# Routing work moved to the end of each step, and residual rows gathered for the last six output tiles

## The chip, the cores and the metric

The kernel runs on one core of a Trainium2 chip. The metric is the device time of one execution in microseconds; three runs were taken. A core has five engines with queues of their own: PE (matrix products, into the PSUM banks), ACT (scalar functions and copies), DVE (elementwise and reductions), POOL (here above all the indirect DMAs, which gather or scatter rows by a list of indices) and SP (which only starts DMAs). They meet at semaphores: an instruction can raise one when it ends, and a queue can wait until one has reached a value. Each queue works strictly in the order in which it is written, so what stands behind a waiting instruction waits too.

## The reference

The input is x of 32 x 64 rows of 128 floats (2048 rows). Three blocks are each added to the residual x:

```python
x = x + xattn(layernorm(x), ctx_1024, ctx_1024, mask, ...)      # 16 heads, 128 context rows
x = x + attn(layernorm(x), A, Wb, bb, Wc, bc, Wd, bd, ...)      # a cumulative-sum recurrence, 32 hidden
x = x + ffn(layernorm(x), routers, W1, W2)                      # 4 layers over a shared pool of 16 experts

def _unipool_layer(xt, router, W1, W2):
    logits = xt @ router                       # (2048, 16)
    probs = softmax(logits)
    w, idx = max(probs), argmax(probs)
    # for each of the 16 experts: silu(xt @ W1[e]) @ W2[e], kept where idx == e, times w
```

W1[e] is 128 x 512 and W2[e] is 512 x 128. The four layers of the last block run one after the other, each with its own router; there is no residual between them. Only the sum at the very end adds the residual.

## The kernel before

Attention fills the span up to about 150 us and the recurrence the stretch up to about 190 us; the change touches neither. The rest is the expert block.

**Tiles, pieces and steps.** Each layer holds the 2048 rows sorted by expert in 16 tiles of 128. A tile that straddles two experts is computed once for each, so the loop runs over `PIECES` = 16 + 15 = 31 pieces (one tile with one expert each). `piece_steps` calls `step(i)` for i = 0 to 32 on every engine. Piece j passes through a pipeline: in step j ACT copies the expert's W1 into a staging buffer (L587); in step j+1 PE multiplies it with the tile (L915, "the hidden product" below), ACT takes the tanh (L599), DVE forms the gated hidden rows (L1300, "h(j)" below); in step j+2 PE multiplies by W2 (L933) and DVE adds the result into the tile's rows, weighted by whether the piece counts (L1316, "y(j)" below). Both products use two banks in turn: the hidden product of piece j needs h(j-2) done, and the second product of piece j needs y(j-2) done. Tile t is final after y(t+15).

**Routing beside it.** In layers 0 to 2 the finished tiles are already routed for the next layer. In step i PE transposes tile i-18 (L883, which waits for y(i-3)), ACT copies it out (L575), and PE multiplies with the router (L851). The 16 tiles are routed in five parts of 4, 3, 3, 3 and 3 tiles. `ending(k)` names the part whose last tile is k. For each part come: `largest` on DVE (L1155, L1159) at the end of the step in which its last tile's router product comes; `exponentials` on ACT (L557, one small instruction for each tile) in the step after; `choose` and `weigh` on DVE (L1167 to L1179, seven instructions); `ranks` on PE (L834, L847, which count rows of each expert); `put` on DVE (L1194 to L1197), which gives each row its place; and then POOL scatters the part's tiles into `expert_rows` in DRAM (L389). `ranks` of a part also waits for `put` of the part before. Parts 0 to 3 fall into the steps; part 4 comes after them. The parts' `exponentials`, `choose` and `weigh` stand in steps 22, 25, 28 and 31, their `ranks` and `put` in steps 23, 26, 29 and 32.

**Between the layers.** After the last `put`, DVE works out the sources of the sorted rows, and POOL gathers them tile by tile (L406) once all scatters have landed.

**The end.** In layer 3 nothing is routed. `finish(t)` on DVE (L1288) in step t+17 multiplies the finished tile by its gate into `yrows[0]`, and POOL adds its 128 rows into the output with one scatter each (L430, `compute_op=ALU.add`); the residual was stored into the output earlier by one plain DMA.

**SP.** Before the expert block SP clears 12 of the 16 parts of `expert_rows`; the last four (4 MB) it clears in layer 0, once 8 tiles of that layer have been transposed (`sp.wait_ge(s["xT_mm"], NT // 2)`).

Of the kernel before, what the change touches and what calls it, by code (L numbers as in the profile page):

```python
# [10 lines left out]
ALU = mybir.AluOpType  # L11
# [11 lines left out]
def perceiver_block(nc, x, ctx, mask, Wq, bq, Wk, bk, Wv, bv, Wo, bo, A, Wb, bb, Wc, bc, Wd, bd,  # L23
# [18 lines left out]
    FIRST = 4  # L42
    PARTS = [(0, 4), (4, 7), (7, 10), (10, 13), (13, 16)]
# [15 lines left out]
    with ExitStack() as stack:  # L59
# [3 lines left out]
        def sem(name):  # L63
            return stack.enter_context(nc.semaphore(name))
# [105 lines left out]
        scored = [sem(f"scored{r}") for r in range(4)]  # L170
        gathered = [sem(f"gathered{t}") for t in range(NT)]
# [40 lines left out]
        def ending(tile):  # L212

            return [b for b, (a, z) in enumerate(PARTS) if z - 1 == tile]

# [25 lines left out]
        def _(sp):  # L241
# [33 lines left out]
            sp.wait_ge(s["xT_mm"], NT // 2)  # L275
# [6 lines left out]
        def _(pool):  # L282
# [138 lines left out]
            def finish_rows():  # L421

                for t in range(NT):
                    pool.wait_ge(gathered[t], L * 16)
                g.tensor_copy(token_i[:], xin[:, :, ID]).then_inc(s["token_ready"], 1)
                pool.wait_ge(s["token_ready"], 1)
                pool.wait_ge(s["x2_stored"], 16)
                for t in range(NT):
                    pool.wait_ge(s["out_row"], t + 1)
                    g.indirect_dma_start(  # L430
                        out=out_rows, out_offset=bass.IndirectOffsetOnAxis(ap=token_i[:, t:t + 1], axis=0),
                        in_=yrows[0][:, t, 0:D], in_offset=None, compute_op=ALU.add).then_inc(s["out_scattered"], 16)
                pool.wait_ge(s["out_scattered"], 16 * NT)
# [13 lines left out]
        def _(act):  # L447
# [123 lines left out]
            def evac_yT(layer, t):  # L571
                act.wait_ge(s["yT_mm"], layer * NT + t + 1)
                if t >= 2:
                    act.wait_ge(s["logits_done"], (layer + 1) * NT + t - 1)
                a.copy(yT[:, t % 2, :], banks[0][:, 0:P]).then_inc(s["yT_evac"], 1)  # L575

            def one_layer(layer):
# [3 lines left out]
                def step(i):  # L581
# [9 lines left out]
                    if routes:  # L591
                        for b in ending(i - 19):
                            exponentials(layer + 1, b)
# [7 lines left out]
                    if routes and 0 <= i - 18 < NT - 1:  # L601
                        evac_yT(layer, i - 18)

# [11 lines left out]
        def _(pe):  # L615
# [252 lines left out]
            def one_layer(layer):  # L868
# [26 lines left out]
                def step(i):  # L895
# [27 lines left out]
                    if routes:  # L923
                        for b in ending(i - 20):
                            ranks(r, b)
# [10 lines left out]
                    if routes and 0 <= i - 18 < NT - 1:  # L936
                        logits_y(i - 18)

# [13 lines left out]
        def _(dve):  # L952
# [324 lines left out]
            def one_layer(layer):  # L1277
# [7 lines left out]
                def finish(t):  # L1285

                    dve.wait_ge(s["y_ready"], count(t + E))
                    v.tensor_scalar(yrows[0][:, t, 0:D], yrows[layer % 2][:, t, 0:D], xin[:, t, GATE:GATE + 1], None,  # L1288
                                    ALU.mult).then_inc(s["out_row"], 1)

                def step(i):
# [10 lines left out]
                    if routes:  # L1302
                        for b in ending(i - 19):
                            choose(r, b)
                            weigh(r, b)
                        for b in ending(i - 20):
                            put(r, b)
# [10 lines left out]
                    if routes:  # L1318
                        for b in ending(i - 18):
                            largest(r, b)  # L1320
                    elif 0 <= i - 17 < NT:
                        finish(i - 17)

                piece_steps(step)
                if routes:
                    largest(r, 4)
                    choose(r, 4)
                    weigh(r, 4)
                    put(r, 4)
# [42 lines left out]
```

## Time and profile before

| | us |
|---|---|
| median of 3 runs | 589.2 |
| lowest and highest run | 586.32, 591.73 |
| the profiled execution | 582.74 |
| its span, first to last instruction | 581.0 |
| mean granted PE clock of the profiled execution | 0.930 |
| busy PE, DVE, ACT, POOL | 492.7, 337.3, 294.8, 193.6 |

The profiled execution was itself quicker than the three timed runs. The span is 1.7 us less than its device time. A clock of 1.00 is 2.4 GHz, 0.50 is 1.2 GHz.

### The profile page before, as it was taken

What the parts mean: (1) busy time and instruction counts of PE and PEld (TensorE: products, weight loads), DVE (VectorE), ACT (ScalarE), POOL (GpSimd) and SP (SyncE); (2) the same over time, 40 slices, a digit from 0 to 9 for tenths busy, and PEclk for the clock granted to TensorE, in tenths of its full rate; (3) what the DMA queues carried; (4) which work ended last, traced back from release to release, by engine and by line L of the source; (5) the groups of instructions that cost most, each with busy time, mean ns of one, the idle gap of its engine ahead of it and who ended that gap; (6) DMA issues with size and microseconds to landing.
All of it is one profiled execution on the core that took longest, in us unless ns stands there. A gap on an engine that the chain in (4) does not pass through costs nothing.

```text
span 581.0 us, 16450 instructions
## 1 busy us (share of the span) xinstructions
PE 492.7 (85%) x5865; PEld 417.4 (72%) x5865; DVE 337.3 (58%) x912; ACT 294.8 (51%) x785; POOL 193.6 (33%) x238
## 2 busy tenths in 40 slices
PE   1689999999788879898778999787799887889992
PEld 1367777777655639897773998774699786479991
DVE  3467877787558674444436654555455445465672
ACT  1277776777571526554421665440466543166660
POOL 8342333231030035302235530233551042563385
PEclk9999999999898789998877999896899989799996
DMA  5643223300089734500001100000110000111143
GB/s 141 184 121 94 64 79 94 94 3 4 3 317 387 265 94 143 214 1 20 16 26 36 43 17 2 20 29 23 44 34 6 3 33 15 34 46 27 11 38 27
DMA packets 39052, 41.43 MB, mean 71 GB/s; under 512 B 5056, under 2 KB 26944, under 8 KB 38976
## 3 DMA queue, kind: packets, MB, share of 16 engines
q1 hardware_dynamic: 31024, 30.68, 16.1%
q0 software_dynamic: 5888, 8.63, 6.7%
q10 hardware_dynamic: 2064, 1.08, 0.7%
q8 instruction: 51, 0.84, 0.6%
q14 instruction: 25, 0.20, 0.1%
HBM read 16.65 MB, written 23.72 MB: 69 GB/s over the span
## 4 chain that ended last, share of the span: by engine, by line
PE 57%; DVE 16%; POOL 8%; issue 7%; ACT 7%; DMA 3%; DVEq 1%; ACTq 0%; POOLq 0%
PE bank L933 17%; PE bank L915 14%; PE bank L710 6%; PE bank L691 4%; POOL out_dram L430 4%; PE bank L669 3%; DVE pp L1300 2%; ACT pp L599 2%; DVE ppT L1045 2%; DVE yrows L1316 2%; PE bank L663 1%; DMA xin<-expert_rows,source_i 1%; PE bank L650 1%; PE bank L639 1%; PE bank L883 1%
## 5 line engine op out<-in xcount | busy, mean ns | idle before, releaser
L1300 DVE SCALAR_TENSOR_TENSOR pp<-pp,bank 128x512 f32<-128x512 f32 x124 | 85.2, 687 | 109.5 <-ACT pp L599 109.5
L933 PE MATMUL bank<-w,pp 128*128 x992 | 143.0, 290 | 4.4 <-issue 2.3
L915 PE MATMUL bank<-vm,ppT 128*128 x992 | 140.5, 286 | 0.1
L933 PEld LDWEIGHTS bank<-w,pp 128*128 128x128 f32 x992 | 127.7, 201 | 10.1 <-issue 7.4
L915 PEld LDWEIGHTS bank<-vm,ppT 128*128 128x128 f32 x992 | 125.5, 198 | 1.1 <-issue 0.6
L599 ACT ACTIVATE pp<-bank 128x512 f32<-128x512 f32 x124 | 74.2, 598 | 98.0 <-PE bank L915 98.0
L389 POOL DMA_INDIRECT expert_rows<-yrows,place_i x48 | 46.6, 972 | 150.4 <-DVE place_i L1197 140.3
L587 ACT COPY ppT<-w 128x512 f32 x124 | 76.6, 618 | 35.6 <-DVE piece_tile L1264 31.6
L492 ACT ACTIVATE pp<-bank,nmax 128x128 f32<-128x128 f32 x256 | 67.8, 424 | 0.0
L406 POOL DMA_INDIRECT xin<-expert_rows,source_i x48 | 46.2, 963 | 37.2 <-PE bank L904 25.7
L1316 DVE SCALAR_TENSOR_TENSOR yrows<-bank,wpiece,yrows 128x128 f32 x124 | 43.1, 347 | 24.4 <-PE bank L933 18.9
L764 PE MATMUL bank<-trib,onesb 128*128 128x512 bf16 x192 | 53.0, 438 | 0.0
L1030 DVE TENSOR_REDUCE nmax<-bank 128x4 f32<-128x512 f32 x64 | 41.0, 684 | 11.4 <-PE bank L669 11.4
L691 PE MATMUL bank<-ident,pp 128*128 128x128 f32 x256 | 40.8, 282 | 7.3 <-DVE ppT L1045 5.7
L331 POOL TENSOR_TENSOR qm<-qT,own_head 128x256 f32<-128x256 f32 x32 | 18.9, 613 | 83.3 <-ACT kT L482 83.3
L764 PEld LDWEIGHTS bank<-trib,onesb 128*128 128x128 bf16 x192 | 21.0, 112 | 25.9 <-issue 10.4
L691 PEld LDWEIGHTS bank<-ident,pp 128*128 128x128 f32 x256 | 27.4, 141 | 14.7 <-ACT pp L492 8.5
L500 ACT COPY ppT<-bank 128x512 f32<-128x512 f32 x32 | 18.9, 589 | 33.6 <-PE bank L691 33.6
L883 PE MATMUL bank<-ident,yrows 128*128 128x128 f32 x48 | 15.4, 320 | 20.6 <-DVE yrows L1316 20.6
L406 POOL DMA_INDIRECT xin<-token_rows,source_i x16 | 15.5, 969 | 51.6 <-DVE source_i L1244 39.2
L430 POOL DMA_INDIRECT out_dram<-yrows,token_i x16 | 25.0, 1560 | 16.2 <-DVE yrows L1288 11.6
L575 ACT COPY yT<-bank 128x128 f32<-128x128 f32 x48 | 12.8, 267 | 29.7 <-PE bank L883 29.7
(205 smaller groups left out, 653.7 us busy)
## 6 DMA issues: line engine op xcount, KB each, us to landing
expert_rows<-zero_rows SPq DMA_DIRECT2D x16, 1056.0 KB, 11.7
w<-in_L_ffn_W_dram SPq DMA_DIRECT2D x32, 256.0 KB, 3.4
cx<-in_ctx_dram SPq DMA_DIRECT2D x16, 128.0 KB, 2.5
token_rows<-yrows ACTq DMA_DIRECT2D x1, 1056.0 KB, 6.7
out_dram<-xs SPq DMA_DIRECT2D x1, 1024.0 KB, 13.9
xs<-in_x_dram SPq DMA_DIRECT2D x1, 768.0 KB, 5.7
expert_rows<-yrows,place_i POOLq DMA_INDIRECT x48, 2.3
xin<-expert_rows,source_i POOLq DMA_INDIRECT x48, 2.6
```

Source lines behind the costliest of these rows:

```text
L389: g.indirect_dma_start(out=region, out_offset=bass.IndirectOffsetOnAxis(ap=place_i[:, t:t + 1], axis=0), in_=yrows[(r + 1) % 2][:, t, :], ...
L406: g.indirect_dma_start(out=xin[:, t, :], out_offset=None, in_=token_rows if layer == 0 else region, in_offset=bass.IndirectOffsetOnAxis(ap ...
L430: g.indirect_dma_start(out=out_rows, out_offset=bass.IndirectOffsetOnAxis(ap=token_i[:, t:t + 1], axis=0), in_=yrows[0][:, t, 0:D], in_off ...
L492: last = a.activation(pp[:, r, k * T:(k + 1) * T], banks[r][:, k * T:(k + 1) * T], ACT.Exp, bias=nmax[:, r, k:k + 1], scale=1.0)
L587: a.copy(w1_piece[:, i % 2, :], w1[:, ds(e * FF, FF)]).then_inc(s["w1_staged"], 1)
L599: a.activation(th[:, j % 2, :], banks[2 + j % 2][:, :], ACT.Tanh, scale=0.5) \
L691: last = nc.tensor.transpose(bank[:, k * P:(k + 1) * P], pp[:, r, k * P:(k + 1) * P], ident[:])
L764: mm(bank[:, :].rearrange("p (k t) -> p k t", k=4), onesb[:], trib[:].unsqueeze(1).broadcast_to([P, 4, P]), start=True, stop=True)
L915: last = mm(banks[2 + j % 2][:, c * P:(c + 1) * P], w1_piece[:, j % 2, c * P:(c + 1) * P], xT[:, ds(tile_of[j] * P, P)], start=True, stop= ...
L933: last = mm(banks[6 + j % 2][:, 0:D], hh[:, j % 2, c * P:(c + 1) * P], w2[:, ds(e * FF + c * P, P)], start=(c == 0), stop=(c == FC - 1))
L1300: v.scalar_tensor_tensor(hh[:, j % 2, :], th[:, j % 2, :], 1.0, banks[2 + j % 2][:, :], ALU.add, ALU.mult).then_inc(s["h_ready"], 1)
L1316: v.scalar_tensor_tensor(sorted_tile, banks[6 + j % 2][:, 0:D], wpiece[:, j:j + 1], sorted_tile, ALU.mult, ALU.add).then_inc(s["y_ready"], 1)
```

## The change

Three things change.

1. In the steps of layers 0 to 2 the routing operations move to the end of the step. On ACT `exponentials` goes behind the tanh and the copy of the transposed tile. On DVE `choose` and `weigh` go behind y, and `put` goes behind them and one step later (steps 24, 27, 30; for part 3, behind the last step). On PE `ranks` goes behind the second product and the router's product.
2. In layer 3, tiles 10 to 15 (`ADDED` = 10): POOL gathers each tile's residual rows from the output into `yrows[0]`, each gather after y(t-1) and all before the first scatter. `finish` adds them (one scalar_tensor_tensor in place of the tensor_scalar), and the tile's scatter writes without adding. Tiles 0 to 9 are as before.
3. SP waits for 14 transposes in place of 8 before it clears the last four parts.

```diff
+    ADDED = NT - 6
@@ sync
-            sp.wait_ge(s["xT_mm"], NT // 2)
+            sp.wait_ge(s["xT_mm"], NT - 2)
@@ gpsimd, finish_rows
-                for t in range(NT):
+                for t in range(ADDED, NT):
+                    pool.wait_ge(s["y_ready"], (L - 1) * PIECES + t)
+                    g.indirect_dma_start(
+                        out=yrows[0][:, t, 0:D], out_offset=None, in_=out_rows,
+                        in_offset=bass.IndirectOffsetOnAxis(ap=token_i[:, t:t + 1], axis=0)) \
+                        .then_inc(x2_gathered[t], 16)
+                for t in range(ADDED):
                     pool.wait_ge(s["out_row"], t + 1)
                     g.indirect_dma_start(
...
+                for t in range(ADDED, NT):
+                    pool.wait_ge(s["out_row"], t + 1)
+                    g.indirect_dma_start(
+                        out=out_rows, out_offset=bass.IndirectOffsetOnAxis(ap=token_i[:, t:t + 1], axis=0),
+                        in_=yrows[0][:, t, 0:D], in_offset=None).then_inc(s["out_scattered"], 16)
@@ scalar, step(i)
-                    if routes:
-                        for b in ending(i - 19):
-                            exponentials(layer + 1, b)
                     if 0 <= i - 1 < PIECES:
...
                     if routes and 0 <= i - 18 < NT - 1:
                         evac_yT(layer, i - 18)
+                    if routes:
+                        for b in ending(i - 19):
+                            exponentials(layer + 1, b)
@@ tensor, step(i)
-                    if routes:
-                        for b in ending(i - 20):
-                            ranks(r, b)
                     if 0 <= i - 2 < PIECES:
...
                     if routes and 0 <= i - 18 < NT - 1:
                         logits_y(i - 18)
+                    if routes:
+                        for b in ending(i - 20):
+                            ranks(r, b)
@@ vector, finish(t)
+                    if t >= ADDED:
+                        dve.wait_ge(x2_gathered[t], 16)
+                        v.scalar_tensor_tensor(yrows[0][:, t, 0:D], yrows[layer % 2][:, t, 0:D],
+                                               xin[:, t, GATE:GATE + 1], yrows[0][:, t, 0:D], ALU.mult, ALU.add) \
+                            .then_inc(s["out_row"], 1)
+                    else:
...
@@ vector, step(i)
-                    if routes:
-                        for b in ending(i - 19):
-                            choose(r, b)
-                            weigh(r, b)
-                        for b in ending(i - 20):
-                            put(r, b)
                     if 0 <= i - 2 < PIECES:
...
                     if routes:
                         for b in ending(i - 18):
                             largest(r, b)
+                        for b in ending(i - 19):
+                            choose(r, b)
+                            weigh(r, b)
+                        for b in ending(i - 21):
+                            put(r, b)
...
                 piece_steps(step)
                 if routes:
+                    put(r, 3)
                     largest(r, 4)
```

DVE's queue before, steps 22 and 23 of layer 0, from h(21) (L1300) through `choose` and `weigh` to h(22) and the first instruction of `put`; L223 loads the tile's number into a register for the y that follows:

```order
L1300 SCALAR_TENSOR_TENSOR pp<-pp,bank 128x512
L1167 TENSOR_REDUCE mx<-ex 128x4
L1168 TENSOR_TENSOR eq<-ex,mx 128x64
L1170 SCALAR_TENSOR_TENSOR nth<-not_first,eq 128x64
L1171 SCALAR_TENSOR_TENSOR ohb<-nth,eq 128x64
L1177 TENSOR_REDUCE sm<-ex 128x4
L1178 RECIPROCAL sm<-sm 128x4
L1179 SCALAR_TENSOR_TENSOR yrows<-mx,sm 128x4
L223 TENSOR_LOAD piece_tile
L1316 ISA
L1316 SCALAR_TENSOR_TENSOR yrows<-bank,wpiece,yrows 128x128
L1300 SCALAR_TENSOR_TENSOR pp<-pp,bank 128x512
```

The same place now (line numbers are those of the changed kernel, h is L1319 and y is L1329):

```order
L1319 SCALAR_TENSOR_TENSOR pp<-pp,bank 128x512
L225 TENSOR_LOAD piece_tile
L1329 ISA
L1329 SCALAR_TENSOR_TENSOR yrows<-bank,wpiece,yrows 128x128
L1180 TENSOR_REDUCE mx<-ex 128x4
L1181 TENSOR_TENSOR eq<-ex,mx 128x64
L1183 SCALAR_TENSOR_TENSOR nth<-not_first,eq 128x64
L1184 SCALAR_TENSOR_TENSOR ohb<-nth,eq 128x64
L1190 TENSOR_REDUCE sm<-ex 128x4
L1191 RECIPROCAL sm<-sm 128x4
L1192 SCALAR_TENSOR_TENSOR yrows<-mx,sm 128x4
L1319 SCALAR_TENSOR_TENSOR pp<-pp,bank 128x512
```

y(20) stood behind the seven instructions and now stands ahead of them; h(22) now follows them directly.

DVE's queue before at the end of layer 0: the `put` of part 3 (L1194 to L1197), y(30), then `largest` of part 4:

```order
L1194 TENSOR_TENSOR rk<-bank,ohb 128x48
L1196 TENSOR_REDUCE place<-rk 128x3
L1197 CAST place_i<-place 128x3
L223 TENSOR_LOAD piece_tile
L1316 ISA
L1316 SCALAR_TENSOR_TENSOR yrows<-bank,wpiece,yrows 128x128
L1155 TENSOR_REDUCE nmx<-bank 128x3
L1159 TENSOR_TENSOR nmx<-nmx,xin 128x3
```

The same place now:

```order
L225 TENSOR_LOAD piece_tile
L1329 ISA
L1329 SCALAR_TENSOR_TENSOR yrows<-bank,wpiece,yrows 128x128
L1207 TENSOR_TENSOR rk<-bank,ohb 128x48
L1209 TENSOR_REDUCE place<-rk 128x3
L1210 CAST place_i<-place 128x3
L1168 TENSOR_REDUCE nmx<-bank 128x3
L1172 TENSOR_TENSOR nmx<-nmx,xin 128x3
```

The last y of the layer no longer stands behind the `put` of part 3.

## Rows read from the trace of the kernel before

**Rows 1.** DVE in order of time, layer 1, steps 21 and 22: start, duration, engine, line.

```profile
359.10 0.69 DVE L1300 SCALAR_TENSOR_TENSOR pp<-pp,bank 128x512 f32<-128x512 f32 x1 [1.28 <-ACT pp L599]
...
362.11 0.69 DVE L1300 SCALAR_TENSOR_TENSOR pp<-pp,bank 128x512 f32<-128x512 f32 x1 [1.68 <-ACT pp L599]
362.71 0.21 DVE L1167 TENSOR_REDUCE mx<-ex 128x4 f32<-128x64 f32 x1
...
364.70 0.35 DVE L1316 SCALAR_TENSOR_TENSOR yrows<-bank,wpiece,yrows 128x128 f32 x1 [0.39 <-issue]
```

**Rows 2.** ACT in order of time, the same steps.

```profile
358.47 0.60 ACT L599 ACTIVATE pp<-bank 128x512 f32<-128x512 f32 x1 [1.00 <-PE bank L915]
...
359.11 0.63 ACT L587 COPY ppT<-w 128x512 f32 x1
360.46 1.13 ACT L557 ACTIVATE ex<-bank,nmx,xin 128x16 f32<-128x16 f32 x4 [0.72 <-DVE nmx L1159]
```

**Rows 3.** PE in order of time, layer 1, steps 21 to 24.

```profile
357.30 1.14 PE L915 MATMUL bank<-vm,ppT 128*128 x8
358.27 0.27 PE L883 MATMUL bank<-ident,yrows 128*128 128x128 f32 x1
358.44 1.15 PE L933 MATMUL bank<-w,pp 128*128 x8
...
359.57 1.14 PE L915 MATMUL bank<-vm,ppT 128*128 x8
...
365.11 0.33 PE L883 MATMUL bank<-ident,yrows 128*128 128x128 f32 x1 [1.44 <-DVE yrows L1316]
...
365.72 1.15 PE L933 MATMUL bank<-w,pp 128*128 x8
...
366.85 2.04 PE L915 MATMUL bank<-vm,ppT 128*128 x8
```

**Rows 4.** Stretches: length, busy (instructions) of PE, PEld, DVE, ACT, POOL; clock, DMA share.

```profile
260.50:296.01 35.51, 30.24 (x226) 27.96 (x224) 16.61 (x58) 16.13 (x43) 9.74 (x10) 0.86 0.06 20
359.10:391.29 32.19, 27.26 (x226) 24.81 (x224) 16.72 (x59) 16.12 (x43) 9.74 (x10) 0.95 0.07 23
455.81:489.46 33.65, 28.71 (x226) 26.41 (x224) 16.56 (x58) 16.13 (x43) 9.74 (x10) 0.90 0.07 22
379.33:388.54 9.21, 7.73 (x73) 6.98 (x71) 5.08 (x19) 4.79 (x13) 2.84 (x4) 1.00 0.07 22
323.72:342.68 18.96, 18.96 (x173) 18.96 (x172) 11.94 (x30) 12.70 (x31) 9.54 (x10) 1.00 0.14 34
228.50:242.20 13.70, 11.42 (x88) 10.15 (x87) 5.23 (x11) 7.28 (x16) 4.39 (x6) 1.00 0.91 334
```

**Rows 5.** The same view, from h(30) to y(30) in layers 0, 1, 2.

```profile
296.01:302.00 5.99, 3.54 (x30) 3.31 (x29) 2.86 (x13) 0.39 (x2) 0.97 (x1) 0.72 0.01 3
391.29:397.28 5.99, 3.51 (x30) 3.31 (x29) 2.86 (x13) 0.39 (x2) 0.96 (x1) 0.74 0.00 0
489.46:495.09 5.63, 3.20 (x30) 2.98 (x29) 2.86 (x12) 0.39 (x2) 0.97 (x1) 0.83 0.00 0
```

**Rows 6.** In order of time, the end of layer 1: the last two `put` and POOL's last scatters.

```profile
395.73 0.17 DVE L1197 CAST place_i<-place 128x3 int32<-128x3 f32 x1
...
402.98 0.97 POOL L389 DMA_INDIRECT expert_rows<-yrows,place_i  x1 [3.29 <-DVE place_i L1197]
```

**Rows 7.** In order of time, POOL and DVE at the end of layer 3.

```profile
546.34 1.65 POOL L430 DMA_INDIRECT out_dram<-yrows,token_i  x1 [11.62 <-DVE yrows L1288]
...
574.32 1.55 POOL L430 DMA_INDIRECT out_dram<-yrows,token_i  x1 [0.30 <-issue]
...
544.00 0.29 DVE L1288 TENSOR_SCALAR yrows<-yrows,xin 128x128 f32<-128x128 f32 x1
...
570.55 0.32 DVE L1288 TENSOR_SCALAR yrows<-yrows,xin 128x128 f32<-128x128 f32 x1
```

**Rows 8.** DMA issues of the page: out, in, queue, count, us from issue to landing.

```profile
expert_rows<-yrows,place_i POOLq DMA_INDIRECT x48, 2.3
...
out_dram<-yrows,token_i POOLq DMA_INDIRECT x16, 3.3
```

More of the change, by code:

```diff
@@ L170, in perceiver_block @@
         scored = [sem(f"scored{r}") for r in range(4)]
+        x2_gathered = [sem(f"x2_gathered{t}") for t in range(NT)]
         gathered = [sem(f"gathered{t}") for t in range(NT)]
@@ L1287, in finish @@
                     dve.wait_ge(s["y_ready"], count(t + E))
-                    v.tensor_scalar(yrows[0][:, t, 0:D], yrows[layer % 2][:, t, 0:D], xin[:, t, GATE:GATE + 1], None,
-                                    ALU.mult).then_inc(s["out_row"], 1)
+                    if t >= ADDED:
[4 more added lines that the diff above has]
+                    else:
+                        v.tensor_scalar(yrows[0][:, t, 0:D], yrows[layer % 2][:, t, 0:D], xin[:, t, GATE:GATE + 1],
+                                        None, ALU.mult).then_inc(s["out_row"], 1)
                 def step(i):
```

## The prediction, written before the changed kernel was run

> **What bounds the kernel now.** I read the stages first (the view of stretches), then each engine's queue in order of time in one routed part of layer 1, then the end. In a stretch of layer 1 without routing PE is busy for 18.96 of 18.96 us at a clock of 1.00 [rows 4]: PE alone bounds it, and what DVE or ACT do there is free. In the routed steps, too, PE bounds an undisturbed step: the hidden product starts at 357.30 and the next one at 359.57, so a step is **2.27 us** [rows 3]. Ten such steps (from h(20) to h(30)) would be 22.7 us, yet they take 35.51, 32.19 and 33.65 us in layers 0, 1 and 2 [rows 4]. Two things fill the difference. First a loop of waits: the exponentials wait for DVE's maximum and hold up the tanh behind them, so h(21) comes at 362.11 instead of 359.10 + 2.27 = 361.37 [rows 1, 2]; then y(20) waits behind choose and weigh until 364.70 [rows 1], and PE's transpose of the next tile waits 1.44 us for it [rows 3]. Second the clock: a hidden product that takes 1.14 us takes 2.04 us at 366.85 [rows 3], just behind that pause, and the mean clock of the three stretches is 0.86, 0.95 and 0.90 [rows 4]. From h(30) to y(30), at the end of each routed layer, another 5.99, 5.99 and 5.63 us pass [rows 5]. At the very end POOL bounds: 16 adding scatters at (574.32 - 546.34) / 15 = 1.865 us each [rows 7], while the tiles are final by 570.55 + 0.32.
>
> **The routed steps.** I replay step 22 with the new order, in units of the trace. Let T be the start of h(21), now 361.37. The tanh starts 0.63 earlier (358.47 against 359.10) and the work after the yT copy starts 0.64 after the tanh (359.11 - 358.47) [rows 1, 2], so the exponentials run from T to T + 1.13 [rows 2]. y(20) is done by T + 1.0. Choose and weigh take from 362.71 to 364.70 - 0.39 = 364.31, 1.60 us [rows 1], and now run from T + 1.13 to T + 2.73. h(22) is due at T + 2.27 and comes 0.46 late; PE needs it only at its second product, which starts 358.44 + 2.27 - 359.10 = 1.61 us after h is due and so about 0.9 us after h's 0.69 us are over [rows 1, 3]. The transpose behind y(21) is the tighter one: y(21) ends at T + 3.68, the transpose is due at 358.27 + 4.54, T + 3.71. So 0.46 is covered, and the other routed part of PE, the ranks, covers more: between transpose and second product there are 0.61 us with ranks and 0.17 without [rows 3], so ranks cost 0.44 of PE. The W1 copy behind the exponentials is ready at about T + 1.8, its product is due at 359.57 + 4.54 = 364.11, T + 2.7. If that cover were gone, each of the nine groups would pay the 0.46. `put` (three short ones) falls into a step with no choose, where DVE waits 1.28 us for the tanh anyway [rows 1]. Ten steps then take 22.7 + 3 x 0.44 = 24.0 us in each layer, 72.0 in three, against 101.35 in sum [rows 4]: **29.3 us less**. Of this the waits are the smaller part that I am sure of: a group of three steps at full clock takes 9.21 [rows 4] against 3 x 2.27 + 0.44 = 7.25, so 1.96 x 9 groups, and the three last steps at (391.29 - 388.54) - 2.27 = 0.48, together **19.1**; the other **10.2** are the clock.
>
> **The clock.** The 2.04 us product follows a pause of PE [rows 3]; the unrouted stretch has no pause and no dip [rows 4]. I therefore take the dips inside the steps as caused by the pauses, and both go. The Trainium skill (TensorE: Matmul & The Clock Gate, "HAM oscillation — how this bites in real kernels") has a rule that speaks against this: its example of a clock that falls is a PE that waits for a DMA between any two groups of products, which these steps do not; by it the dips would not be these waits' doing, would stay, and the time would be that of rival B. The same page ("A second HAM failure mode: psum-queue depth-cycling") also has a clock that swings under short pauses between groups of products, which is what the trace shows.
>
> **The end of a routed layer.** With T the start of h(30): y(29) by T + 1.0, exponentials to T + 1.13, choose and weigh to T + 2.73, the register load of y(30) 0.39 [rows 1], so y(30) starts at T + 3.12. The second product needs only y(29) and h(30) and is done by about T + 2.4. Against 17.61 us in three layers [rows 5] that is 9.4: **8.2 us less**. Behind y(30) now come `put` of part 3 and three scatters. Before, that `put` started its last instruction at 395.73, 1.55 before y(30), and POOL was idle 3.29 us before the last part's scatters [rows 6]; now it ends about 1.1 to 1.4 us behind y(30), some 2.8 later, and 0.5 of the 3.29 remains. It costs nothing, but if the ranks of part 3 are late by more than 0.5, POOL's three scatters of 0.97 + 0.30 are the next to be late: bound 1.1 us a layer, 3.3 in all. On the other side PE enters the end at full clock; up to 0.9 a layer, 2.7 in all, by the 2.04 against 1.14. I take neither.
>
> **Layer 3.** Six scatters without adding: the same kind takes 0.97 [rows 6] and 0.30 between [rows 7]. The eleventh starts at 574.32 - 5 x 1.865 = 565.0, the last at 565.0 + 5 x 1.27 = 571.35; the last tile is ready at 570.55 + 0.35 (the duration of y, the same kind of operation on the same shape [rows 1]) + 0.26 = 571.2, so it waits hardly. That is 3.0 us, and landing may be 3.3 - 2.3 = 1.0 shorter [rows 8], of which I count half: **3.5 less**. Both ends: a first adding scatter started 2.05 us after its tile was ready (544.00 + 0.29 against 546.34) [rows 7], and if a change of kind costs as much, 1.8 of it is lost: 1.2 to 4.0. The Trainium skill (DMA: Bandwidth & Descriptors, "Anatomy of one DMA — SWDGE (gpsimd) path") gives one time for every such DMA, 2.0 us and the bytes over 436e3 per us, 2.15 us for 64 KB as an estimate; that fits the 2.3 and not the 3.3, and by it landing would gain nothing and the term would be 3.0. The six gathers (6 x 1.27 = 7.6 us) lie in POOL's 11.62 us of idle time before the first scatter [rows 7], each released by a y; the last is free by about 543.6. The first finish that waits for one comes ten finishes of 1.77 (570.55 - 544.00 over 15) after 544.00, some 15 us later. DVE does the six finishes in 0.35 instead of about 0.30 us, beside PE's work.
>
> **The clears.** While the last four parts are cleared, 13.70 us at 334 GB/s, PE is busy 11.42 only [rows 4], with steps 3 us long instead of 1.9. They now start six steps later, about 238, and end about 252, still before the routed steps (layer 0's begin at 260.50) and the scatters into the region behind them. The loss moves and stays: 0, within 1 either way.
>
> **Sum.** 29.3 + 8.2 + 3.5 = 41.0 us. From the profiled execution's own 582.74 that leaves 541.7. The median of the runs is 6.5 us above that execution; I carry the difference over: 589.2 - 41.0 = **548**.
>
> **The rivals.**
> - A, all as above: 548, 540 to 553 with the bounds of each term. Chance 0.60.
> - B, the dips of the clock stay though the waits go: 589.2 - 30.8 = 558. For it: the clock also dips between layers whatever the routing does. Against: the unrouted stretches. Chance 0.24.
> - C, DVE's chain takes the place of the old one: choose and weigh stand wholly in front of the next h, so each of nine groups pays 1.60 and half of the clock's gain and of the layer ends' goes with it. 41 - 14.4 - 5.1 - 4.1 = 17: 572. Against: h waits 1.28 us for the tanh in every step. Chance 0.10.
> - D, the other side: PE works on without a pause through the routed steps too, and the granted clock falls under this unbroken work. A step at half clock costs 2 x (2.04 - 1.14) = 1.8 us more [rows 3]; from 23 of the 30 routed steps on, the 41 are used up, and with all 30 the time is 589.2 - 41 + 54 = 602. Against it stands the unrouted stretch at 1.00 [rows 4]. Chance 0.03.
> - E, the change doesn't do what it says: `ranks` waits for the `put` before, which is a step later now, and this rebuilds the loop. The order leaves two steps between the two, so only a late `put` would do it; then nothing is won but the end, 585. Chance 0.03.
>
> **Chances and range.** One per cent is 5.9 us, about what a measurement of this kernel can tell from none. A, B and C are all beyond it: faster 0.94; same 0.03 (E); slower 0.03 (D). The range takes A with its bounds and B with 8 us for the spread of runs: 539 to 566.
>
> **What would show it.** Right: in the profile after, h follows h at 2.27 (2.7 in a step with ranks) from h(20) to h(30), 24 us a layer; PE's idle time before the transpose of y (L883 before) nearly gone; the clock of those stretches 1.00; h(30) to y(30) about 3.1; the last scatter starting near the time of the last finish. Wrong: exponentials or the W1 copy ahead of a late hidden product (C), products of 2 us without a pause before them (B, D), or POOL's idle time gone before the last part's scatters while the gathers wait for them.

## The result, and the profile after

| | before | after |
|---|---|---|
| median on the same chip, four runs each | 587.88 | 557.46 |
| lowest and highest | 586.32, 591.73 | 555.56, 558.14 |
| the profiled execution | 582.74 | 558.14 |
| its span | 581.0 | 556.4 |
| mean granted PE clock | 0.930 | 0.965 |

The ratio is 0.947, with a 95% interval of 0.941 to 0.952: 30.4 us faster by the medians. Forecast were 41.0 us and 548, with a range of 539 to 566.

I read the stages first, with the same borders as before: h(20) to h(30) of layers 0, 1 and 2, then h(30) to y(30). The columns are those of [rows 4].

```profile
260.10:287.02 26.92, 24.78 (x223) 22.55 (x222) 16.49 (x58) 14.84 (x40) 6.97 (x8) 1.00 0.06 19
349.24:376.10 26.86, 24.92 (x224) 22.56 (x223) 16.49 (x59) 14.95 (x40) 6.99 (x8) 1.00 0.06 19
438.34:465.44 27.10, 24.93 (x223) 22.63 (x222) 16.57 (x58) 14.83 (x40) 6.98 (x8) 1.00 0.06 19
287.02:289.95 2.93, 2.27 (x26) 1.99 (x24) 2.27 (x9) 1.17 (x5) 2.32 (x3) 1.00 0.14 46
376.10:379.12 3.02, 2.26 (x26) 1.98 (x25) 2.28 (x10) 1.16 (x5) 2.41 (x3) 1.00 0.14 45
```

The clock is 1.00 in all of them; in [rows 4] it was 0.86, 0.95 and 0.90. The layer ends fell from 5.99 [rows 5] to 2.93 and 3.02. But the ten routed steps take 26.9 us, not the 24.0 of the forecast. One step carries most of that difference. Here it is in layer 1 (h(24) at 358.72, h(25) at 361.07, h(26) at 365.64), from the timeline of DVE, ACT, PE and POOL:

```profile
359.17 1.02 POOL L391 DMA_INDIRECT expert_rows<-yrows,place_i  x1 [26.74 <-DVE place_i L1210]
...
360.49 1.00 POOL L391 DMA_INDIRECT expert_rows<-yrows,place_i  x1 [0.30 <-issue]
...
361.07 0.69 DVE L1319 SCALAR_TENSOR_TENSOR pp<-pp,bank 128x512 f32<-128x512 f32 x1
...
361.79 0.97 POOL L391 DMA_INDIRECT expert_rows<-yrows,place_i  x1 [0.30 <-issue]
...
361.88 1.14 PE L928 MATMUL bank<-vm,ppT 128*128 x8
362.84 0.35 DVE L1329 SCALAR_TENSOR_TENSOR yrows<-bank,wpiece,yrows 128x128 f32 x1 [1.08 <-PE bank L943]
363.07 0.96 POOL L391 DMA_INDIRECT expert_rows<-yrows,place_i  x1 [0.30 <-issue]
...
365.01 0.60 ACT L609 ACTIVATE pp<-bank 128x512 f32<-128x512 f32 x1 [3.38 <-remote]
...
365.64 0.69 DVE L1319 SCALAR_TENSOR_TENSOR pp<-pp,bank 128x512 f32<-128x512 f32 x1 [2.45 <-ACT pp L609]
```

The hidden product starts at 361.88 and takes 1.14, so the tanh is due at about 363.0. It comes at 365.01, with a releaser that the profile calls "remote". The step takes 4.57 us, and 4.64 and 4.56 in layers 0 and 2. Beside it stand the four scatters of part 0, back to back.

Layer 3 lost time too: from the last y of layer 2 (468.37) to its own last y (549.57) it takes 81.20 us, against 75.07 before. Its middle, in the order of time:

```profile
513.47 0.95 POOL L432 DMA_INDIRECT yrows<-out_dram,token_i  x1 [1.87 <-issue]
...
514.72 0.94 POOL L432 DMA_INDIRECT yrows<-out_dram,token_i  x1 [0.30 <-issue]
...
515.97 0.94 POOL L432 DMA_INDIRECT yrows<-out_dram,token_i  x1 [0.30 <-issue]
516.76 1.06 PE L928 MATMUL bank<-vm,ppT 128*128 x8
517.21 0.94 POOL L432 DMA_INDIRECT yrows<-out_dram,token_i  x1 [0.30 <-issue]
518.41 0.60 ACT L609 ACTIVATE pp<-bank 128x512 f32<-128x512 f32 x1 [3.02 <-issue]
...
520.86 1.67 PE L928 MATMUL bank<-vm,ppT 128*128 x8
...
522.32 1.91 PE L943 MATMUL bank<-w,pp 128*128 x8
```

The new residual gathers stand back to back, the tanh waits 3.02 us, PE pauses for 2.05 us (until 519.87), and behind that two products take 1.67 and 1.91 us; the granted clock from 520.90 to 524.50 is 0.53 on average. The end of the span:

```profile
540.55 1.55 POOL L438 DMA_INDIRECT out_dram<-yrows,token_i  x1 [0.30 <-issue]
542.41 0.99 POOL L443 DMA_INDIRECT out_dram<-yrows,token_i  x1 [0.30 <-issue]
...
550.58 0.96 POOL L443 DMA_INDIRECT out_dram<-yrows,token_i  x1 [0.57 <-DVE yrows L1303]
```

The last scatters now wait for DVE, where in [rows 7] DVE's tiles waited for POOL. From the last y to the end 6.85 us pass; they were 10.84.

The profiled executions differ by 24.6 us, and the stretches add up to that: routed steps -20.5, layer ends -8.7, the end of the span -4.0, layer 0 up to h(20) -0.4, last y to h(20) of the next layer +2.2 and +0.7, layer 3 +6.1.

### The profile page after: what moved, and what is told of

Its sections match the earlier page's. It is cut to its first block, busy times and chain, and to the rows that moved or that the text cites. A ratio compares the mean times of both kernels' runs of the same rounds, so it can differ in the third digit from the quotient of the medians.

```text
span 556.4 us, 16462 instructions
## 1 busy us (share of the span) xinstructions
PE 479.8 (86%) x5865; PEld 403.8 (73%) x5865; DVE 337.7 (61%) x912; ACT 292.9 (53%) x785; POOL 195.6 (35%) x244
## 4 chain that ended last, share of the span: by engine, by line
PE 67%; DVE 9%; issue 7%; ACT 6%; POOL 5%; DMA 3%; another core or an unknown queue 2%; ACTq 0%; DVEq 0%; POOLq 0%
PE bank L943 21%; PE bank L928 19%; PE bank L723 6%; PE bank L704 5%; PE bank L682 3%; POOL expert_rows L391 3%; DVE ppT L1058 2%; PE bank L864 2%; PE bank L676 1%; PE bank L917 1%; PE bank L663 1%; PE bank L652 1%; DMA xin<-expert_rows,source_i 1%; DMA expert_rows<-yrows,place_i 1%
## 5 line engine op out<-in xcount | busy, mean ns | idle before, releaser
L943 PE MATMUL bank<-w,pp 128*128 x992 | 138.3, 283 | 12.3 <-DVE pp L1319 5.8
L1319 DVE SCALAR_TENSOR_TENSOR pp<-pp,bank 128x512 f32<-128x512 f32 x124 | 85.2, 688 | 103.2 <-ACT pp L609 96.5
L928 PE MATMUL bank<-vm,ppT 128*128 x992 | 138.8, 283 | 0.4 <-issue 0.2
L943 PEld LDWEIGHTS bank<-w,pp 128*128 128x128 f32 x992 | 122.1, 194 | 21.3 <-issue 17.5
L928 PEld LDWEIGHTS bank<-vm,ppT 128*128 128x128 f32 x992 | 123.8, 196 | 1.4 <-issue 0.9
L1329 DVE SCALAR_TENSOR_TENSOR yrows<-bank,wpiece,yrows 128x128 f32 x124 | 43.1, 348 | 17.7 <-PE bank L943 16.3
L777 PE MATMUL bank<-trib,onesb 128*128 128x512 bf16 x192 | 50.9, 426 | 0.0
L1058 DVE COPY ppT<-bank 128x512 f32<-128x512 f32 x32 | 20.7, 686 | 9.9 <-PE bank L723 9.6
L603 ACT COPY vm<-bank 128x128 f32<-128x128 f32 x64 | 17.1, 267 | 17.5 <-PE bank L917 16.6
L917 PE MATMUL bank<-ident,xin 128*128 128x128 f32 x64 | 18.3, 286 | 8.3 <-DVE xin L1225 5.0
```

What stands on the lines that cost most here:

```text
L777: mm(bank[:, :].rearrange("p (k t) -> p k t", k=4), onesb[:], trib[:].unsqueeze(1).broadcast_to([P, 4, P]), start=True, stop=True)
L928: last = mm(banks[2 + j % 2][:, c * P:(c + 1) * P], w1_piece[:, j % 2, c * P:(c + 1) * P], xT[:, ds(tile_of[j] * P, P)], start=True, stop= ...
L943: last = mm(banks[6 + j % 2][:, 0:D], hh[:, j % 2, c * P:(c + 1) * P], w2[:, ds(e * FF + c * P, P)], start=(c == 0), stop=(c == FC - 1))
L1319: v.scalar_tensor_tensor(hh[:, j % 2, :], th[:, j % 2, :], 1.0, banks[2 + j % 2][:, :], ALU.add, ALU.mult).then_inc(s["h_ready"], 1)
L1329: v.scalar_tensor_tensor(sorted_tile, banks[6 + j % 2][:, 0:D], wpiece[:, j:j + 1], sorted_tile, ALU.mult, ALU.add).then_inc(s["y_ready"], 1)
```

## The experiments

All times are medians. Each group of runs had its own runs of the kernel before beside it, with a median of 587.88 beside the changed kernel, 591.08 beside the runs on the ranks, the spaced scatters, layer 3 and the clears, 592.05 beside those on no three in a row, the paced gathers, the start and all three, 588.38 beside the two edits and the first and last burst runs shown, and 591.18 beside the bursts of 4, 3 and 2. So 2 or 3 us between medians of different groups say little, and the steps in the traces say more. The theory that they test, **G**: three or more indirect DMAs issued back to back by POOL hold up the other engines for up to 2 us. Its rivals: **P**, the new place of `ranks` on PE makes the slow step; and for layer 3, **N**, the gathers are not to blame.

**The place of ranks.**

```diff
 transpose_y(i - 18)
+for b in ending(i - 20): ranks(r, b)
 ... second product, logits_y
-for b in ending(i - 20): ranks(r, b)
```

> The changed kernel with one part of the change undone: on PE, ranks stands ahead of the second product again, as before. In the profile of the changed kernel h(26) comes 4.57 us behind h(25) in each routed layer (2.27 would be undisturbed), y(24) comes about 1.1 us late and the tanh of step 27 about 2.2 us late. Theory P (the place of ranks on PE makes this): with ranks ahead, the 4.57 falls to about 2.7, the time falls by 3 x 1.9, about 5 to 6 us (to 552); but the transpose and second product of the step with ranks come 0.44 us later. Theory G (four back-to-back scatters on POOL hold up the other engines while they are issued): the 4.57 stays wherever PE's ranks stand, time the same within 2 us, or slightly slower by up to 3 x 3 x 0.44 = 4. If ranks ahead rebuilds the old loop with put (which is now a step later) the pauses grow to those of the kernel before: up to 20 us slower.

Measured: 569.94 (566.98 to 572.91), 12.5 us slower than the changed kernel in another group and 11.8 slower than the nearly equal kernel of the clears in its own. The slow step stays: 4.69, 4.71 and 4.70 us. **P is refuted.** The price of the place is higher than G expected: the routed stretches take 29.08, 29.94 and 30.58 us, the layer ends 4.4. DVE's `choose` now ends later in the step, and with `ranks` ahead the second product waits for it (in part 0's step PE stands idle for 0.56 us before `ranks`, released by the `ohb` that `choose` writes). So the PE part of the change carries a gain of its own, some 12 us. This kernel also shows the stall best (layer 0; PE, then who waits for it):

```profile
273.45 1.15 PE L946 MATMUL bank<-w,pp 128*128 x8 [0.31 <-issue]
...
274.59 1.14 PE L928 MATMUL bank<-vm,ppT 128*128 x8
...
277.29 0.35 DVE L1329 SCALAR_TENSOR_TENSOR yrows<-bank,wpiece,yrows 128x128 f32 x1 [3.36 <-remote]
277.30 0.60 ACT L609 ACTIVATE pp<-bank 128x512 f32<-128x512 f32 x1 [3.49 <-remote]
```

y waits for the first of these products, the tanh for the second. PE makes them one after the other, yet both waits end within 0.01 us of each other.

**The scatters spaced.**

```diff
 for t in range(a, z):
+    if r > 0 and b < 3 and t > a:
+        pool.wait_ge(s["y_ready"], (r - 1) * PIECES + z + 19 + t - a)
     g.indirect_dma_start(out=region, ...)
```

> The changed kernel, with the scatters of parts 0, 1 and 2 spaced out: each scatter after the first of its part waits for one y more, so that they come one per step (2.27 us) and not back to back (1.27 us). Theory G (POOL's burst of scatters stalls the others): the step of 4.57 us in each routed layer falls to about 2.3 to 2.7, each routed layer is about 2 to 3 us shorter, the time falls by 5 to 8 us (to 550 to 552). Theory P (the place of ranks on PE): nothing moves, 557 within 1; the scatters of the last parts start no earlier and no later, since parts 3 and 4 are issued as before.

Measured: 555.68 (551.39 to 556.44). The step h(25) to h(26) fell to 2.45 in all three layers, but a step of 4.02 to 4.05 us appeared at h(27) to h(28). At that place the last scatter of part 0 runs into those of part 1, so that three stand close together. In layer 1 (the tanh due at about 369.9):

```profile
366.98 0.97 POOL L393 DMA_INDIRECT expert_rows<-yrows,place_i  x1 [1.30 <-DVE yrows L1331]
...
368.25 0.97 POOL L393 DMA_INDIRECT expert_rows<-yrows,place_i  x1 [0.30 <-issue]
369.82 0.97 POOL L393 DMA_INDIRECT expert_rows<-yrows,place_i  x1 [0.60 <-issue]
371.39 0.60 ACT L611 ACTIVATE pp<-bank 128x512 f32<-128x512 f32 x1 [2.01 <-remote]
```

The time alone said little: 2 us between the medians, or 5 by the ratios to the kernel before (0.938 against 0.947). The slow step followed the burst, and that was the lead.

**No three in a row.**

```diff
-    if r > 0 and b < 3 and t > a:
-        pool.wait_ge(s["y_ready"], (r - 1) * PIECES + z + 19 + t - a)
+    if b < 3 and (t > a or b == 1):
+        pool.wait_ge(s["y_ready"], (r - 1) * PIECES + z + 19 + t - a + (b == 1))
```

> The changed kernel with the scatters of parts 0 to 2 spaced as in the run before (one y each), and in addition the three of part 1 each one y later, so that no three scatters follow each other directly before the layer's last y. With the scatters spaced but part 1 directly behind part 0, three stood back to back and the slow step moved from h(25)-h(26) (4.57 us) to h(27)-h(28) (4.02 us). Theory G (three or more back-to-back indirect DMAs on POOL hold up the others): that 4.02 falls to about 2.6, the stretch h(20) to h(30) from 25.7 to about 24.2, 4.5 us in all: 551. Rival (about 1.5 us are lost once in each routed stretch wherever it falls, POOL's order has nothing to do with it): a step of 4 us stays somewhere in the stretch, 555.7 as in the run before.

Measured: 549.76 (546.76 to 553.87). No step of 4 us is left. The windows h(20) to h(30) of the three layers:

```profile
261.17:285.15 23.98, 23.69 (x223) 22.24 (x222) 16.39 (x58) 14.74 (x40) 6.85 (x7) 1.00 0.06 19
346.55:370.56 24.01, 23.74 (x223) 22.24 (x222) 16.40 (x59) 14.75 (x40) 6.87 (x7) 1.00 0.06 19
431.89:456.25 24.36, 23.94 (x223) 22.31 (x222) 16.53 (x59) 14.79 (x40) 6.86 (x7) 1.00 0.06 19
```

That is the **24.0 us** of the prediction, and PE is busy for 23.7 of them. The rival (a loss of 1.5 us that stays somewhere in the stretch) is refuted. Against the changed kernel h(20) to h(26), with part 0's scatters, is 2.1 to 2.2 us shorter in each layer, and h(26) to h(30), with part 1's, 0.7.

But the edit does not quite do what was expected of it. Part 1's last scatter now comes so late that part 2's first two follow it directly. In layer 1, around h(30) at 370.56:

```profile
369.63 0.97 POOL L393 DMA_INDIRECT expert_rows<-yrows,place_i  x1 [1.66 <-DVE yrows L1331]
...
370.91 0.97 POOL L393 DMA_INDIRECT expert_rows<-yrows,place_i  x1 [0.30 <-issue]
...
372.19 0.97 POOL L393 DMA_INDIRECT expert_rows<-yrows,place_i  x1 [0.31 <-issue]
...
374.13 0.35 DVE L1331 SCALAR_TENSOR_TENSOR yrows<-bank,wpiece,yrows 128x128 f32 x1 [1.08 <-PE bank L945]
```

From h(30) to y(30) it takes 3.56 to 3.57 us here, against 2.93 to 3.02 in the changed kernel. So of the 8.5 us won in the routed steps 1.8 are lost again at the layer ends.

**The layer 3 part alone undone.** The diff is one line, `ADDED = NT` for `NT - 6`.

> The changed kernel without the second part of the change: all 16 tiles are scattered with adding, nothing is gathered in layer 3 (the routing order and the later clears stay). In the two profiles the end (last y to the end of the span) went from 10.84 to 6.83 us, while y(30) of layer 2 to y(30) of layer 3 went from 75.07 to 81.20. Theory M (the six gathers stall the middle of layer 3, 4 of the 6.1 us: a stall of 2.2 at 515.4 to 518.4 and 1.8 of half clock behind it): here the middle gets 4 back and the end loses 4, the time is that of the changed kernel within 1 us (557). Theory N (the middle's loss has nothing to do with the gathers): the time is 3.5 to 4 us longer, 561, and layer 3 still takes about 81.

Measured: 560.69 (557.41 to 561.99), 2.6 slower than the kernel of the clears beside it. The middle is free of loss without the gathers: h(14) to h(18) of layer 3 take 7.14 us at a clock of 1.00, against 11.09 at 0.85 (changed kernel, then this one):

```profile
514.91:526.00 11.09, 9.04 (x67) 8.86 (x66) 4.64 (x10) 4.32 (x9) 5.87 (x6) 0.85 0.18 38
```

```profile
517.79:524.93 7.14, 7.14 (x66) 7.14 (x66) 4.37 (x10) 4.41 (x9) 0.25 (x1) 1.00 0.01 2
```

The end costs 10.85 again. The time is the 561 of N, but layer 3 takes 77.60 us and not N's 81, and its middle is free: the trace refutes N, not the time. M's cause is right. Between these two profiles its balance of zero holds in layer 3 (3.9 back, 4.0 lost), while by the medians this kernel is 2.6 to 3.2 us slower than the two others. The loss isn't the same each time: in the six profiles with the unspaced gathers these four steps take 8.1, 8.2, 9.0, 11.1, 11.6 and 11.8 us. On average they lose 2.8 us against 7.15, while the gain of 4.0 at the end is there in each.

**The clears.** `sp.wait_ge(s["xT_mm"], NT // 2)` in place of `NT - 2`.

> The changed kernel with SP's wait as before (the last four parts are cleared after 8 transposes, not after 14). The prediction had this move at 0 within 1 us either way: the loss of steps 3 us long beside the 334 GB/s moves by six steps and keeps its size. Same time within 1 us (557); in the profile the steps of 3 us of layer 0 are those at 228 to 240 again. Rival: one of the two places overlaps with something that the other doesn't (the layer's own gathers), then 1 to 2 us either way.

Measured: 558.14 (555.97 to 559.90), the same, and the steps of 3 us are back at h(8) to h(10). Nothing gained or lost that the spread of the runs would show, as predicted.

**Four paced gathers.**

```diff
-    ADDED = NT - 6
+    ADDED = NT - 4
-    pool.wait_ge(s["y_ready"], (L - 1) * PIECES + t)
+    pool.wait_ge(s["y_ready"], (L - 1) * PIECES + 10 + 2 * (t - ADDED))
```

> The changed kernel with four tiles in place of six in the second part of the change (ADDED = 12), and their four gathers in layer 3 spaced by two y each (3.6 to 3.8 us) in place of back to back. In the changed kernel five of the six gathers come within 8 us (510.63, 513.47, 514.72, 515.97, 517.21) and h(14) to h(18) of layer 3 take 11.09 us in place of 7.16 (13 of the 16 adding scatters alone, without gathers: 7.16). Theory M with G: the four steps take 7.16 again, 3.9 us less; at the end twelve adding scatters end 11 x 1.865 behind the first (about 523.4), at 544, before the last tiles are ready, so the end stays at 6.8: 553.5. Rival (any gather beside the layer, not the burst, costs): 1 us a gather stays, 557 or little less.

Measured: 555.95 (554.68 to 556.06). The four steps take 7.15 us, as expected. But the end takes 7.31, not 6.8: with twelve adding scatters POOL is the last again by half a microsecond. The median gained 1.5 us, or nearly 5 by the ratios to the kernel before (0.939 against 0.947); what this edit is worth in the whole time stays open between the two.

**The start of a layer.**

```diff
-    elif t >= 4:
+    elif t >= 3:
...
-        pool.wait_ge(s["xT_mm"], layer * NT + t - 3)
+        pool.wait_ge(s["xT_mm"], layer * NT + t - 2)
```

> The changed kernel; at each layer's start POOL gathers tile t once tile t-3 has been transposed (t-4 in the changed kernel), from t = 3 on (t = 4). In the changed kernel seven gathers follow each other directly and h(0) to h(3) take 7.51, 7.20, 7.64 and 7.40 us in layers 0 to 3, in place of 5.7. Theory G: with fewer in one burst the loss of 1.5 to 1.9 us in each layer falls or goes: up to 6 us less, 551 to 557. Against: the first four or five still come within 6 us, and a tile that comes later than PE needs it costs up to 1 us a layer: up to 4 us more.

Measured: 558.06 (556.37 to 560.02), no gain. Layers 0 and 3 start better (h(0) to h(3) 5.5 and 6.1 us), but new steps of 2.5 to 3.2 us appear at h(5), h(9) and h(11). G doesn't hold as a rule here: in the kernel of 549.76 us layers 1 and 2 pass the same gathers almost without a loss (first steps 2.14 and 2.12), and layer 3 loses 1.4. The kernel before issues the same gathers too, six of them 1.25 to 1.5 us apart, and takes 5.55, 5.62 and 5.73 us from h(0) to h(3) in layers 0, 1 and 3, and 7.01 only in layer 2.

**All three, and two of them.**

> The three edits of this group together: scatters of parts 0 to 2 never three in a row, four paced residual gathers, the layer start with three tiles in flight. By theory G the gains add: 557.5 - 6 (scatters) - 4 (gathers) - 0 to 6 (start) = 541 to 548. If they don't add (the same microseconds lost at another place), 552.

> The changed kernel with two of the three edits of the kernel of 546.05 us: scatters of parts 0 to 2 spaced, four paced residual gathers; the layer's start as in the changed kernel. The three tiles in flight alone gave 558.06 (nothing against 557.46), and moved small losses to other steps. Theory: it gives nothing here either, 546 within 2 (549.8 - 4 for the middle of layer 3 = 545.8). Rival: it helps once the rest is spaced: 549 or more without it.

Measured: 546.05 (544.48 to 552.81, five of the six at most 547.93) and **545.32** (542.38 to 546.89), the ratio of the second to the kernel before 0.927 (0.924 to 0.930). The gains add up (7.7 and 1.5 us alone, 12.1 together, all between medians of different groups), and the start's edit adds nothing. The spaced scatters with the four paced gathers beat both kernels, the changed one by 12 us.

**The burst by itself.** Into the kernel of 545.32 us I put DMAs that nobody needs, behind y(14) of layers 0 to 2, where POOL is idle; the spare gathers' results are not used.

```diff
+def extra(layer):
+    ...
+    n = (2, 3, 4)[layer]
+    pool.wait_ge(s["y_ready"], layer * PIECES + 15)
+    for k in range(n):
+        g.indirect_dma_start(out=spare[:, k, :], in_=token_rows, ... token_i[:, k:k + 1] ...)
```

> The kernel of the two edits, and in the unrouted stretch of layers 0, 1 and 2, behind y(14), POOL makes 2, 3 and 4 indirect gathers that nobody needs, back to back, 64 KB each, into a spare tile (their results aren't used). There a step takes 1.79 us without exception, PE is busy without a pause, and POOL has nothing else to do. It measures the disputed cost by itself. Theory G: with 2 nothing, with 3 or 4 one step of the layer takes 1.5 to 2.3 us longer, as in the routed steps (4.57 against 2.35 with four, 4.02 against 2.35 with three). Rival R (the burst hurts only where the scatters read yrows and PE, ACT and DVE wait for each other as in the routed steps): all steps stay at 1.79.

> As the run with 2, 3 and 4 unneeded gathers in layers 0, 1 and 2, but with 4, 3 and 2. There the step h(17) to h(18) took 2.51, 3.05 and 4.47 us (2.66, 2.73 and 2.72 in layers 0, 1 and 2 without a burst). Theory G (the number of back-to-back gathers makes it): now about 4.4, 3.05 and 2.7. Rival (it is the layer, so the place in the program or the code, and the number is by chance in step with it): about 2.5, 3.05 and 4.5 again.

> As the run before, with other work on POOL at the same place: in layer 0 four plain DMAs of 128 rows from POOL's queue back to back, in layer 1 four memsets of 128 x 512 (about 0.45 us each, from 1.85 us for 128 x 2112), in layer 2 four indirect gathers, but one per step. Theory G with the indirect DMA's issue as its cause: all three stay at 1.79 per step. If POOL's being busy is enough, layer 1 shows a longer step; if any burst of DMAs is, layer 0 does.

The two steps from h(17) to h(19) without a burst, as windows of layers 0 to 2:

```profile
252.82:257.83 5.01, 5.01 (x44) 4.68 (x44) 2.08 (x4) 2.55 (x7) 0.00 (x0) 1.00 0.01 3
337.98:342.98 5.00, 5.00 (x44) 4.74 (x44) 2.04 (x4) 2.54 (x7) 0.00 (x0) 1.00 0.00 0
423.87:428.87 5.00, 5.00 (x44) 4.74 (x43) 2.04 (x4) 2.55 (x7) 0.00 (x0) 1.00 0.02 3
```

With 2, 3 and 4 gathers:

```profile
252.07:256.85 4.78, 4.78 (x43) 4.53 (x42) 2.04 (x4) 2.56 (x7) 0.00 (x0) 1.00 0.02 4
338.21:343.48 5.27, 5.26 (x43) 4.81 (x43) 1.99 (x4) 2.53 (x7) 1.30 (x2) 1.00 0.11 26
424.35:431.05 6.70, 5.26 (x44) 4.82 (x44) 1.99 (x5) 2.55 (x7) 2.25 (x3) 1.00 0.15 34
```

With 4, 3 and 2:

```profile
253.07:259.87 6.80, 5.10 (x43) 4.60 (x42) 2.07 (x5) 2.85 (x7) 1.42 (x2) 1.00 0.13 28
342.44:347.84 5.40, 5.26 (x44) 4.82 (x44) 2.00 (x5) 2.54 (x7) 1.30 (x2) 1.00 0.11 27
429.55:434.74 5.19, 5.14 (x44) 4.79 (x45) 2.08 (x5) 2.54 (x7) 0.36 (x1) 1.00 0.08 18
```

Against the windows without a burst two gathers cost -0.2 to 0.2 us, three 0.3 and 0.4, four **1.7 and 1.8**, in either order of the layers. In the other runs, which have no such DMAs, the same two steps take 4.78 to 5.03 us in layer 0 and 5.00 to 5.19 in layer 2, so the cost of two is none that can be told. It is the number and not the layer. The clock stays 1.00. For three, G's 1.5 is too much here; with three close together in the routed steps (after one more 2.3 us ahead) it was 1.7, and at the layer end of the kernel of 549.76 us 0.6.

R is refuted in one half: these gathers read `token_rows`, not `yrows`. Its other half, that the engines must wait for each other as in the routed steps, this run can't settle, since the slow step, h(17) to h(18), is one in which PE already transposes a finished tile. The middle of layer 3 speaks against it: nothing is routed there, and a step beside the gathers is slow all the same.

With other kinds of work (layer 0: four plain DMAs, layer 1: four memsets, layer 2: four gathers, a wait for one more y ahead of each), POOL's rows and the windows:

```profile
247.48 2.22 POOL L435 DMA_DIRECT2D spare<-token_rows  x4 [10.40 <-DVE yrows L1352]
334.68 1.92 POOL L437 MEMSET curT<- 128x512 f32 x4 [6.68 <-DVE yrows L1352]
```

```profile
250.69:255.47 4.78, 4.78 (x43) 4.53 (x42) 2.03 (x4) 2.54 (x7) 0.00 (x0) 1.00 0.01 3
337.18:342.17 4.99, 4.99 (x44) 4.74 (x44) 2.03 (x4) 2.54 (x7) 0.00 (x0) 1.00 0.00 0
423.37:428.56 5.19, 5.14 (x44) 4.79 (x45) 2.08 (x4) 2.54 (x7) 2.26 (x3) 1.00 0.13 33
```

Nothing but 0.2 us in layer 2. Neither four plain DMAs, nor four memsets, nor the same four gathers spaced out (the first two 1.3 us apart, the others 2.3 to 2.4) make the stall. But the plain DMAs and the memsets kept POOL busy for only 2.22 and 1.92 us, no longer than two gathers, which cost nothing either; four gathers take 4.7. That a POOL kept busy as long by other work would not stall the others is not shown. (The whole kernels took 549.76, 553.20 and 548.50 us, two runs each; their ends are about 2 us longer and their layer starts vary. Only these steps of them are used.)

## Why the prediction was right and where it was wrong

**The direction, and the mechanism of the routed steps: right.** The pauses in which PE waited for y, and the clock dips behind them, are gone together: PE's idle time before the transposes of y falls from 43.6 us to 7.2 in the whole span, and the clock is 1.00 in all routed stretches. That refutes rival B (0.24), by which the dips stay, and D, and C: with the scatters spaced a step behind `choose` takes 2.0 to 2.8 us. The replay's 0.46 us is there as well: the step into which `choose` runs takes 2.71 us, and the one behind it 2.05. E didn't happen. In the run with `ranks` ahead it didn't either, since `ranks` waits there for `choose` and not for a `put`.

The number is another matter. 557.46 lies above the 540 to 553 of A; it is within the range only because that was widened for B, and it falls on B's 558 by chance, since B's mechanism is refuted.

**The routed steps: the term was too large.** Forecast 29.3, measured 20.5 in the profiles. The failing step is "Ten steps then take 22.7 + 3 x 0.44 = 24.0 us": the sum priced PE, ACT and DVE and gave POOL's scatters no price, since none waits for them there. With the same instructions and only the scatters spaced the steps take 23.98, 24.01 and 24.36, 8.5 us less in the three layers than in the changed kernel. So nearly all of the 8.8 us missing are the scatters, some 6.4 those of part 0 and 2.1 those of part 1.

**The layer ends: right.** 8.2 forecast, 8.7 measured. y(30) comes 2.93 to 3.02 behind h(30), forecast 3.12. The point about POOL was right as well, and close. The last `put` of part 3 and what follows on POOL in layer 1:

```profile
380.79 0.17 DVE L1210 CAST place_i<-place 128x3 int32<-128x3 f32 x1
...
381.24 0.97 POOL L391 DMA_INDIRECT expert_rows<-yrows,place_i  x1 [1.75 <-DVE place_i L1210]
...
385.06 0.96 POOL L391 DMA_INDIRECT expert_rows<-yrows,place_i  x1 [0.30 <-DVE place_i L1210]
```

It ends 1.8 us behind y(30), not 1.1 to 1.4, and POOL's idle time before the last part, 3.29 us in [rows 6], is down to 0.30. Of the bound of 1.1 us a layer 0.6, 0.1 and 0.5 came true: from the last y to the next h(0) it takes 18.60, 18.11 and 18.30 us, before 18.00, 18.00 and 17.76. The rest of the 2.9 us that layers 1 and 2 lost up to h(20), 2.2, lies nearly all between their h(0) and h(3). The gathers stand back to back there, but they did so in the kernel before as well, so that this loss is not explained.

**Layer 3: the end right, the middle missed.** 3.5 forecast at the end and 4.0 measured, the upper bound. But "the six gathers lie in POOL's 11.62 us of idle time" stood for a price of nothing, and layer 3 took 6.1 us more up to its last y. 3.9 of it lie at the gathers, 1.7 at the layer's start (h(0) to h(3) 7.39 against 5.73) and 0.5 ahead of it. POOL's own time was free there; that of the engines beside it was not. The Trainium skill (SBUF — State Buffer, "SBUF: two separate sides") says that at the memory's ports a DMA and a compute engine cannot slow each other, and that among the engines only POOL and DVE share a pair of ports. If those ports were all that counts, the gathers should have cost ACT and PE nothing. The runs here don't show at which place the engines are held, but they do show that the cost isn't nothing: four unneeded gathers lengthen two steps from 5.0 to 6.7 us, and the wait that grows is the tanh's, on ACT.

**The clears: right**, nothing.

**The carry-over to the median: wrong by 7 us, in my favour.** The profiled execution before was 5.1 us quicker than the median of its four runs, that of the changed kernel 0.7 slower than its own. By the profiles I was off by 558.14 - 541.7 = 16.4 us; its parts are 8.8 in the routed steps, -0.5 at their ends, -0.5 at the span's end, 2.9 between the layers, 6.1 in layer 3, and -0.4. The carried 6.5 us and the 0.7 hid all but 9.3 of it in the medians. Of the forecast value itself, then, the working was worse than the result shows.

**Open:** by what path the burst works. In the run with `ranks` ahead two products of PE seem to end at the same instant for those who wait, 1.6 to 2.7 us late. That looks like word of PE's completions arriving late and in a bunch, not like PE working slowly; but ends of matmuls are modelled, so it isn't shown. One more trait is steady: in the six profiles with part 0's four scatters back to back, 18 layers in all, the late tanh starts 0.97 to 1.14 us after the fourth scatter has left POOL (in layer 1 of the changed kernel 365.01 against 363.07 + 0.96). So the end of the wait keeps step with the end of the burst, whatever holds it. Open too are why the gathers at a layer's start cost 2 us in some layers and nothing in others, whether the number of indirect DMAs or the length of POOL's unbroken work matters, and how much of the kernel before's loss was this burst and how much the waits.

## What to carry to other kernels

Price a POOL DMA not only on POOL. Here four indirect DMAs in a row, for which nobody waited, held up the others for about 2 us, so such a burst deserves a row in the sum. If the receiver has slack, hang each DMA of a burst on a later semaphore value, and look in the trace whether the bursts have only moved; here a wait in front of the scatters gave 7.7 us between the medians. When a step is slow in every layer at the same place, move the suspect by one step and see whether the slow step moves with it, since the time alone may hide it (555.68 against 557.46).

## What the runs showed of the hardware that I had not expected

- Four indirect gathers of 66 KB (128 rows of 132 floats) issued every 1.25 us lengthened the two steps beside them by 1.7 to 1.8 us, three by 0.3 to 0.4, two by 0.2 at most. Four plain POOL DMAs (0.55 us each to issue), four memsets (0.48 each) and four spaced gathers did not, the first two in a shorter stretch of POOL's time.
- An adding scatter of 128 rows into the output holds POOL for 1.55 us in most cases, one that only writes for 0.96 to 0.99 (both in the changed kernel).
- PE products of 1.67 and 1.91 us in place of 1.06, at a mean granted clock of 0.53, followed a pause of 2.05 us in layer 3, while in the run with `ranks` ahead a pause of 1.97 us inside the routed steps of layer 0 left the clock at 1.00.
